# A grouped attention loop, and another order of the work at its end, in a gated cross-attention and expert layer

## What is computed

```python
x = x + tanh(g_xattn) * attention(layernorm(x), ctx, ctx, mask)   # 16 heads of 64
x = x + tanh(g_ffn)   * experts(layernorm(x))                     # 8 experts, D 128, hidden 512
# attention: q, k, v projections with biases; scores / 8; mask and causal mask to -1e30;
#            softmax; times v; times Wo, plus bo.
# experts:   argmax over softmax(x @ Wr + br) picks one expert per token;
#            for i in range(8): out += relu((x * chosen_i) @ W1[i] + b1[i]) @ W2[i] + b2[i]
```

## Time and profile before

| | us |
|---|---|
| median of 3 runs | 360.89 |
| the runs | 360.82, 364.35, 360.89 |
| the profiled execution | 365.85 |
| its span, first to last instruction | 363.8 |
| a batch of the loop (198.87 to 234.33) | 35.46 |
| end of the loop to the first expert product (273.63 to 306.11) | 32.5 |
| first expert product to the end of the span | 57.7 |

### The profile page before, as it was taken

How to read it: one execution, slowest core, us unless ns; L and a number is a source line. 1 busy time by engine, 2 the same in 40 slices (tenths; PEclk the granted TensorE clock), 3 DMA queues, 4 the chain that set the end, 5 groups by cost and what they waited for, 6 DMA issues and landing times.

```text
span 363.8 us, 11160 instructions
## 1 busy us (share of the span) xinstructions
PE 345.6 (95%) x2835; PEld 283.3 (78%) x2835; DVE 270.9 (74%) x1262; ACT 255.5 (70%) x936; POOL 191.0 (52%) x369
## 2 busy tenths in 40 slices
PE   8999999999999999999999999999999897978893
PEld 6776778778878787878778877887887666968893
DVE  4789995878687868786878687867777696776671
ACT  3686775887687868785878587859773667646562
POOL 7245555366537744774467436833681570345544
PEclk9999999999999999999999999999999999999999
DMA  6999202000400030004000400040005914133320
GB/s 201 248 367 244 91 2 90 4 2 1 122 0 0 0 119 0 0 0 119 0 0 0 119 0 0 17 117 0 0 29 211 366 36 133 50 104 105 89 66 13
DMA packets 21562, 27.87 MB, mean 77 GB/s; under 512 B 3649, under 2 KB 16789, under 8 KB 21536
## 3 DMA queue, kind: packets, MB, share of 16 engines
q1 hardware_dynamic: 19776, 23.85, 21.7%
q0 software_dynamic: 1504, 3.16, 2.5%
q10 hardware_dynamic: 256, 0.56, 0.5%
HBM read 19.00 MB, written 9.01 MB: 77 GB/s over the span
## 4 chain that ended last, share of the span: by engine, by line
PE 80%; DVE 10%; issue 3%; ACT 3%; DVEq 1%; DMA 1%; another core or an unknown queue 1%; POOLq 0%; SPq 0%; POOL 0%; ACTq 0%
PE ps_kv L1255 15%; PE ps_o L1255 13%; PE ps_s L1255 13%; PE ps_t L1359 11%; PE ps_w L1255 10%; PE ps_q L1255 8%; PE ps_t L1255 7%; DVE masked L823 2%; DVE prob_T L842 2%; PE ps_s L1479 1%; ACT prob L565 1%; PE ps_w L1396 1%; DMA nat<-in_ctx 1%; DVE row_fix L830 1%
## 5 line engine op out<-in xcount | busy, mean ns | idle before, releaser
L433 POOL TENSOR_SCALAR prob<-prob,row_inv 128x128 f32<-128x128 f32 (+1 forms) x256 | 104.8, 429 | 124.9 <-DVE row_inv L836 124.7
L565 ACT ACTIVATE prob<-masked,neg_max 128x128 f32<-128x128 f32 (+1 forms) x256 | 113.7, 447 | 65.5 <-DVE neg_max L823 65.2
L823 DVE CUSTOM_DVE_ANT_0 masked<-ps_s,mask_now 128x128 f32<-128x128 f32 (+1 forms) x256 | 77.8, 353 | 44.3 <-PE ps_s L1255 40.8
L842 DVE COPY prob_T<-ps_t 128x384 f32<-128x384 f32 x123 | 65.0, 549 | 0.8 <-PE ps_t L1359 0.7
L1255 PE MATMUL ps_s<-k_T,q_T 64*128 64x128 f32 (+1 forms) x512 | 59.6, 351 | 1.5 <-DVE neg_max L823 1.5
L1359 PEld LDWEIGHTS ps_t<-ident,prob 128*128 128x128 f32 x384 | 41.0, 141 | 21.5 <-issue 17.3
L1359 PE MATMUL ps_t<-ident,prob 128*128 128x128 f32 x384 | 56.1, 282 | 0.6 <-DVE prob_T L842 0.5
L1255 PE MATMUL ps_o<-prob_T,v_nat 128*64 128x256 f32 (+1 forms) x512 | 49.8, 333 | 2.1 <-DVE prob_T L842 1.5
L565 ACT ACTIVATION_READ_ACCUMULATOR prob<-masked,neg_max 128x1 f32 x256 | 48.5, 190 | 0.0
L1255 PEld LDWEIGHTS ps_o<-prob_T,v_nat 128*64 128x64 f32 x512 | 31.7, 136 | 16.3 <-issue 2.1
L1255 PEld LDWEIGHTS ps_s<-k_T,q_T 64*128 64x128 f32 x512 | 33.9, 188 | 9.7 <-issue 6.8
(11 more groups left out here) (200 smaller groups left out, 545.9 us busy)
## 6 DMA issues: line engine op xcount, KB each, us to landing
ctx_buf<-in_ctx SPq DMA_DIRECT2D x8, 768.0 KB
sorted_rows<-pad_rows SPq DMA_DIRECT2D x8, 642.5 KB, 4.4
tile_in<-sorted_rows SPq DMA_DIRECT2D x24, 128.5 KB, 2.1
packs<-in_L_ffn_W SPq DMA_DIRECT2D x1, 2048.0 KB
packs<-in_L_ffn_W SPq DMA_DIRECT2D x8, 256.0 KB
nat<-in_ctx SPq DMA_DIRECT2D x8, 128.0 KB, 3.4
nat<-in_x SPq DMA_DIRECT2D x1, 768.0 KB, 6.6
w_in<-in_L_xattn_Wk SPq DMA_DIRECT2D x2, 256.0 KB, 4.5
```

The lines of the kernel that those rows point to most:

```text
L433: g.tensor_scalar(prob[:, slot, lo:hi], prob[:, slot, lo:hi], row_inv[:, slot, t:t + 1], 1.0, ALU.mult, ALU.mult).then_inc(prob_ready, 1)
L565: s.activation(prob[:, slot, lo:hi], masked[:, slot % 2, lo:hi], ACT.Exp, bias=neg_max[:, slot, t:t + 1], scale=-1.0, accum_out=row_sum[:, ...
L823: v.tensor_tensor_reduce(out=masked[:, slot % 2, lo:hi], in0=ps_s[slot % 2][:, lo:hi], in1=mask_now[:, lo:hi], scale=-SCALE, scalar=FLOOR, ...
L842: v.tensor_copy(prob_T[:, slot % TSLOTS, :], ps_t[slot % 2][:, 0:W3]).then_inc(probT_kept, 1)
```

## The change

In the loop (batches 1 to 6) two pairs are taken together, so a batch has 4 groups g instead of 8 steps j.

- PE: at the end of a group `two_scores` makes the scores of two pairs, right behind the values of two pairs. Before, the scores of each pair stood alone in front of its transposes. Each head's bank `ps_s[h]` now holds all of one pair and the 128-column piece of the next; the 256-column pieces of the next pair go to halves of `ps_kv` and `ps_q` (`ps_s2`). So `project_q` waits for the first and `project_kv` for the second maximum of a group, and the last two products of `two_scores` wait until k, v and q have been copied out.
- DVE: `shared_maxima` first reads these two pieces, then come the other six. The maxima are written straight into `prob`; `masked` is gone, and with it the wait on `exp_done`. DVE copies q of the odd pairs (`keep_q`), ACT that of the even ones. The steps of `second_norm`, `choose` and `place` run in blocks (0 to 4 in group 0, 5 to 11 in group 1, `choose` 0 to 2 and the next mask in group 2, `choose` 3 to 5 and `place` in group 3).
- ACT: `keep_kv` of both pairs and the exponentials of both pairs alternate. The copy of the inputs (`keep_inT`) stands at the end of group 0, and the inputs' transposes go to `ps_w` instead of `ps_q`.
- Batch 0 ends, and the last batch begins, with the matching pieces: the scores of two pairs are made before the output projection.
- The end: of the early second weights only tile 0's stands ahead of the last pair's `keep_probT`; tiles 5 and 6 are copied later. ACT's first weights: three tiles ahead of the last `keep_oT` instead of five. `last_projection(7)` stands ahead of the first tile's transpose. `norm_transposes`, `router` and `ranks` of the last batch stand earlier among PE's tile products, `late_table` is not interrupted, and one `store` instead of two (`SOON`) stands ahead of the last scatter.

```diff
+        ps_s2 = [ps_kv[:, 0:S], ps_q[:, S:2 * S]]
...
+            def loop_batch(b):
+                for g in range(PAIRS // 2):
+                    if g == 2:
+                        sum_context(b + 1)
+                    if g == 3:
+                        residual_of(b)
+                    for i in range(SUMS, SUMS + 2):
+                        for h in range(2):
+                            normalise(8 * b + 2 * g + i, h, (2 * (2 * g + i) + h) % SLOTS)
+                        if g == 3 and i == SUMS:
+                            scatter(b - 1)
...
+                    s.activation(prob[:, slot, lo:hi], prob[:, slot, lo:hi], ACT.Exp,
...
+                for h in heads:
+                    exponential(p + which, h, (2 * (j + which) + h) % SLOTS,
+                                4 * p + (7 + h if which else 4 + 2 * h))
...
+            def loop_batch(b):
+                for g in range(PAIRS // 2):
+                    j, p = 2 * g, 8 * b + 2 * g
+                    a = 8 * b + PAIRS - 2 + j
+                    if g == 0:
+                        context_now(b + 1)
+                    if g == 2:
+                        keep_y(b)
+                    if g == 0:
+                        two_exponentials(p + SUMS, j + SUMS, 0)
+                        two_exponentials(p + SUMS, j + SUMS, 1, (0,))
+                    keep_q(a, a_pair(g))
+                    keep_kv(a, a_pair(g))
+                    if g == 1:
+                        keep_mean(b)
+                    if g == 2:
+                        keep_x2T(b - 1)
+                    if g > 0:
+                        two_exponentials(p + SUMS, j + SUMS, 0)
+                    else:
+                        two_exponentials(p + SUMS, j + SUMS, 1, (1,))
+                    keep_kv(a + 1, a_pair(g) + 1)
+                    if g > 0:
+                        two_exponentials(p + SUMS, j + SUMS, 1)
+                    if g == 0:
+                        keep_inT(b + 1)
+                    for i in range(2):
+                        keep_oT(b, p + i, j + i, p + 2)
...
-            early_w1(5)
+            early_w1(3)
             for tile in range(EARLY):
                 if tile < EARLY - 1:
                     keep_tileT(tile + 1, tile + 1)
-                if tile == 1:
-                    early_w1(6)
+                if tile + 4 < EARLY:
+                    early_w1(tile + 4)
                 act.wait_ge(w1_early, tile + 1)
                 keep_hidden(tile, tile)
...
+            def masked_maximum(slot, t, scores):
+                lo, hi = ((0, P), (P, W3))[t]
+                v.tensor_tensor_reduce(out=prob[:, slot, lo:hi], in0=scores, in1=mask_now[:, lo:hi], scale=-SCALE,
+                                       scalar=FLOOR, op0=ALU.add, op1=ALU.min,
+                                       accum_out=neg_max[:, slot, t:t + 1]).then_inc(max_ready, 1)
...
+            def shared_maxima(p, j):
+                dve.wait_ge(scores_done, p + 2)
+                dve.wait_ge(probT_done, 2 * (p + 2) - SLOTS)
+                settle(dve)
+                for h in (1, 0):
+                    masked_maximum((2 * j + 2 + h) % SLOTS, 1, ps_s2[h])
+            def own_maxima(j, h):
+                for t, (lo, hi) in enumerate(((0, P), (P, W3))):
+                    masked_maximum((2 * j + h) % SLOTS, t, ps_s[h][:, lo:hi])
+            def short_maxima(j):
+                for h in range(2):
+                    masked_maximum((2 * j + 2 + h) % SLOTS, 0, ps_s[h][:, W3:W3 + P])
             def fix_sums(p, slot):
...
+            def keep_q(p, j):
+                dve.wait_ge(q_done, p + 1)
+                v.tensor_scalar(q_T[:, j, :], ps_q[:, 0:S], bias_T[:, j:j + 1], None, ALU.add).then_inc(q_dve, 1)
...
+                    ahead = not (last and (j == 0 or j >= PAIRS - AHEAD)) and not (first and j == PAIRS - 1)
+                    if last and j == 0:
+                        shared_maxima(p + SUMS, SUMS)
+                        for h in range(2):
+                            own_maxima(SUMS, h)
+                        short_maxima(SUMS)
+                        for h in range(2):
+                            keep_probT(p, h, h)
                     if not (last and j >= PAIRS - SUMS):
                         fix_sums(p + SUMS, 2 * (j + SUMS) % SLOTS)
...
+            def loop_batch(b):
+                for g in range(PAIRS // 2):
+                    j, p = 2 * g, 8 * b + 2 * g
+                    shared_maxima(p + SUMS, j + SUMS)
+                    if g > 0:
+                        for h in range(2):
+                            keep_probT(p, h, (2 * j + h) % SLOTS)
+                    for h in range(2):
+                        own_maxima(j + SUMS, h)
+                    if g == 3:
+                        for step in (3, 4, 5):
+                            choose(b - 1, step)
+                    short_maxima(j + SUMS)
+                    if g == 0:
+                        normalise_x(b + 1)
+                        for h in range(2):
+                            keep_probT(p, h, (2 * j + h) % SLOTS)
+                    for h in range(2):
+                        keep_probT(p + 1, h, (2 * j + 2 + h) % SLOTS)
+                    keep_q(8 * b + PAIRS - 1 + j, a_pair(g) + 1)
+                    if g == 3:
+                        for step in range(4):
+                            place(b - 1, step)
+                    fix_sums(p + SUMS, 2 * (j + SUMS) % SLOTS)
+                    invert_sums(p + SUMS, 2 * (j + SUMS) % SLOTS)
+                    for step in ((0, 1, 2, 3, 4), (5, 6, 7, 8, 9, 10, 11), (), ())[g]:
+                        second_norm(b - 1, step)
+                    if g == 2:
+                        for step in range(3):
+                            choose(b - 1, step)
+                        dve.wait_ge(max_ready, 4 * 8 * (b + 1))
+                        mask_of(b + 1)
+                    if g == 3:
+                        sum_context(b + 1)
+                    fix_sums(p + AHEAD, 2 * (j + AHEAD) % SLOTS)
+                    invert_sums(p + AHEAD, 2 * (j + AHEAD) % SLOTS)
...
-            finish(0, 0)
+            early_w2(5)
             dve.wait_ge(x2T_done, B)
             v.tensor_copy(x2_T[:, :], ps_w[:, S:2 * S]).then_inc(x2T_kept, 1)
+            finish(0, 0)
             early_rest(1)
-            finish(1, 1)
             for step in range(6):
                 choose(B - 1, step)
-            early_rest(2)
+            finish(1, 1)
             for step in range(4):
                 place(B - 1, step)
+            early_rest(2)
             finish(2, 2)
-            early_rest(3)
             for step in range(9):
                 late_table(step)
-                if step == 3:
-                    finish(3, 3)
-                    early_rest(4)
+            early_rest(3)
+            finish(3, 3)
+            early_w2(6)
+            early_rest(4)
             finish(4, 4)
             early_rest(5)
...
+                if isinstance(b, int) and b == 1:
+                    all_q_kept(0)
+                else:
+                    pe.wait_ge(x2_ready, 2 * (b - 1))
                 for t in range(QT):
-                    t_.transpose(ps_q[:, t * P:(t + 1) * P], x_norm[:, t, :], ident[:, :])
+                    t_.transpose(ps_w[:, t * P:(t + 1) * P], x_norm[:, t, :], ident[:, :])
                 for t in range(QT):
-                    last = t_.transpose(ps_q[:, S + t * P:S + (t + 1) * P], ctx_now[:, t, :], ident[:, :])
+                    last = t_.transpose(ps_w[:, S + t * P:S + (t + 1) * P], ctx_now[:, t, :], ident[:, :])
...
+            def score(out_, j, h, t):
+                mine = slice(h * DK, (h + 1) * DK)
+                return mm(out_, q_T[mine, j, t * P:(t + 1) * P], k_T[mine, j, 0:(t + 1) * P])
+            def two_scores(p, j, b, nb, nj):
+                pe.wait_ge(k_kept, p + 2)
+                for i in range(2):
+                    q_kept(b, j + i)
+                pe.wait_ge(max_ready, 4 * p)
+                for i, lo in ((0, 0), (1, W3)):
+                    for h in range(2):
+                        score(ps_s[h][:, lo:lo + P], j + i, h, 0)
+                for h in range(2):
+                    score(ps_s[h][:, P:W3], j, h, 1)
+                pe.wait_ge(k_kept, p + 4)
+                pe.wait_ge(v_kept, p + 4)
+                q_kept(nb, nj)
+                for h in range(2):
+                    score(ps_s2[h], j + 1, h, 1).then_inc(scores_done, 1)
...
             def batch(b, first=False, last=False):
+                if last:
+                    for h in range(2):
+                        transpose_probs(8 * b, h, h)
+                    pe.wait_ge(max_ready, 4 * (8 * b + SUMS) + 1)
+                    project_q(b, PAIRS - 2)
+                    pe.wait_ge(max_ready, 4 * (8 * b + SUMS) + 2)
+                    project_kv(b, PAIRS - 2)
...
+            def loop_batch(b):
+                for g in range(PAIRS // 2):
+                    j, p = 2 * g, 8 * b + 2 * g
```

(43 more changed lines are left out.)

134 lines of the change are left out of this document (65 added, 69 removed).

## The result

| | changed kernel | before | ratio |
|---|---|---|---|
| first measurement, 14 runs each | 360.11 us (359.03 to 361.5) | 362.49 us (360.82 to 364.35) | 0.9941 [0.9924, 0.9958] |
| profiled execution, time and span | 359.03 and 357.3 us | 365.85 and 363.8 us | |
| again, second chip | 364.06 us | 364.79 us | 0.9973 [0.9951, 0.9995] |
| again, third chip | 359.59 us | 363.32 us | 0.9902 [0.9879, 0.9924] |

The forecast was 353.3 us, from 360.9, with a range of 348.5 to 359: a gain of 7.6 us. By the three ratios the measured gains are 2.1, 1.0 and 3.6 us. That is no change that counts by the 1% bound, an outcome to which the forecast had given 0.11. In the first profile of the changed kernel five of the six loop batches agree within 0.02 us and one, the second, lies 0.3 above, so a single profile gives the batch time; most of what differs between executions lies outside the loop.

A forecast was written before the change was run, and what follows sets the result against it. PE, busy 95% of the span and throughout a loop batch, was taken as the bound. Loop -5.4, batch 0 +0.3, last batch -1.6 and behind the loop -0.9 took 360.9 to 353.3 us; range 348.5 to 359.

The forecast's parts named there:

- the 1% bound: Whole kernel: about 3.6 us is what a measurement can tell from no change; chance of staying within it 0.11.
- The shapes: PE in the loop: fewer changes of the array's shape around scores and values save 1.9 us a batch.
- lower bound of the saving: PE in the loop: 1.3 us a batch, if the longer score block pays its 0.20 again between its parts.
- The new waits: PE in the loop: scores sharing banks with q and k make it wait 1.2 us a batch, bounds 0.5 and 1.9.
- The ring: Loop, one project_q to the next through ACT, DVE and PE: 7.8 us in group 1, 7.95 in group 2.
- group 3's copy: Loop, group 3: the second copy of prob_T comes 0.1 us late behind choose.
- The ends: Batch 0 up to +0.5, taken +0.3; last batch -1.6; behind the loop -0.9 us.
- After it nothing changes: Behind the loop: past the first late product, itself 0.9 us earlier, nothing more is gained or lost.
- B: Loop: the shared bank costs groups 0 to 2 0.8 us more each; about 361 us, no change; chance 17%.
- C: Behind the loop: the end gives nothing back, loop as forecast; 354.2 us, or 356 without the last batch; chance 11%.
- A: Loop: the ring is covered, waits 0.5 us a batch or less; loop -8.4 and more, 350 us or less; chance 14%.
- upper bound of 1.9 for the waits: Loop: PE's new waits reach 1.9 us a batch if each link takes 0.2 more.

The follow-up runs named there:

- e5: Changed kernel plus one 128-column full-array product between values and scores of each loop group; a loop batch took 36.84 us, against 36.29 with the product ahead of the values.
- e4: Changed kernel without steps 5 to 9 of the second norm in the loop; loop batches took 34.84 to 34.95 us.
- e9: Changed kernel with norm steps spread into VectorE's idle time, router steps 3 to 5 in group 2, empty-row store later; 358.61 us, ratio 0.982 to before.
- e1: Changed kernel with only the second norm's twelve steps spread otherwise over groups 0 and 1; 360.12 us, ratio 0.9879 to before.

## Why the prediction was wrong, point by point

**The shapes: right.** It had 33.4 us without waits; the distances give 33.3. By parts, 0.8 of the 1.9 are in the score visits, 0.3 in the transposes behind them, 0.4 in the small products, and the rest in what no longer stands beside a change. (Its lower bound of the saving, 1.3, is 1.1 by its own price of 0.20 for each of four score blocks.) Score blocks of 16 records take 1.51, and the separate test gives 0.14 to 0.20 for a border priced at 0.16. The Trainium skill, "TensorEngine Tiling (Array Packing)", Key Properties, says that a tiling-mode change drains the engine; e5 shows a cost there. The drain of about 128 cycles that the Trainium skill gives in "TensorE: Matmul & The Clock Gate", Step-by-step, is 53 ns by that estimate and 0.6 us a batch for 11 borders. It is too small beside the 0.14 to 0.20 us of e5 and the 1.9 a batch.

**The new waits: the step that failed, by its size.** The ring was found where it is, with the releasers named; its waits were to be 1.25 us a batch and are 2.2. Term by term, forecast then measured: group 2's query 0.4, 0.85; group 3's query 0.4, 0.37; group 1's, `in_T`, 0.35, 0.46; group 3's copy 0.1, 0.40; group 0 none, 0.09. The ring from group 1's query to group 2's was to take 7.8 and took 8.23 (209.82 to 218.05); the next was to take 7.95 and took 7.90. Two terms make most of it. In group 2, steps 5 to 11 of the norm were taken as 2.3 from their share at the end of the kernel and took 2.76, and the slow restart after a wait, 0.08 to 0.18 each time, had no price. In group 3 the router's steps between the maxima delay the copies of `prob_T` by 0.4, not 0.1. Net 0.9 a batch was the difference of 2.1 and 1.2, so an error of one microsecond in the smaller took all of it. It was also wrong to treat the waits as the price of the shared banks: the batch is 0.65 shorter in e4, with part of the small VectorE work left out, and 0.8 in e9, with it moved.

**The ends: near.** Batch 0 was to lose 0.3 and gained 0.3 to 0.4. The last batch and the end were to give 2.5 and gave 3.1 on a chip without late completions, 0.5 of it behind tile 7, where the clock differed, which the forecast had no term for. By parts: to the last batch's first projection 1.6 forecast, 1.9 measured (18.23 to 16.37); the projection's end 1.0 more, 1.1 measured; the wait of 1.49 for the last pair's copy is gone. The expert table is ready 46.1 us behind the last loop batch's projection (314.45 less 268.37, third profile), before 49.6 (319.49 less 269.87, first profile) or 49.1 (319.70 less 270.60, third): 3.0 to 3.5 earlier, forecast 3.7. Tile 7's product comes 2.6 earlier (50.58 against 53.17), forecast 2.5. "After it nothing changes" held there within 0.5. It did not hold on the second chip, whose profiles have late completions and where nothing of the earlier tile 7 was left at the end; that the one took back the other is likely, but no run there was without them.

**The rivals.** B had the right time, 361 and no change, and its sentence that each late link of VectorE shows is what happened, but not 0.8 in each of three groups: the excess over the forecast is 0.45 before group 2's query, 0.1 before group 1's and 0.3 at group 3's copy. C, an end that gives nothing back, is what one chip shows, for a reason that no rival named. A does not add up: waits of 0.5 a batch give 9.6 us of loop and 349 by the forecast's other terms, not 8.4 and 350; its time of 350 stands for waits of 0.7. With B at 17% and the range ending at 359, the range rested on the upper bound of 1.9 for the waits; 0.2 more at each link was too little, for links that are not in the trace of before.

## What to carry to other kernels

When a change trades work of the bounding engine for waits in a new ring, the gain is the difference of two numbers of like size: price the ring from both sides at full width, and let the range take in zero. A ring's slack is decided by where the small work of the other engines stands, so ask for each such piece whether it lies between the last input and the handover, and move it into that engine's idle time; here that was worth 4.7 us of loop (six times 0.79) where the change itself was worth nothing. The new place has a price too: in e1 it stood behind a scatter, in e9 ahead of a maximum. Before moving a wait's named cause, ask what else its time covered: the transposes that made PE wait for a copy were hiding a maximum.
